# A sparse expert feed-forward: routed pairs only, with the routing of twelve batches inside the cross-attention

## The reference

```python
shared_out = _silu_and_mul(xf @ shared_w1.T) @ shared_w2.T
probs = jax.nn.softmax(xf @ gate_w.T, axis=-1)
routing_weights, selected = jax.lax.top_k(probs, 6)
combine = zeros((T, E)).at[arange(T)[:, None], selected].add(routing_weights)
gate_up = jnp.einsum('th,eoh->teo', xf, w1)
act = _silu_and_mul(gate_up)
moe_out = jnp.einsum('te,tei,ehi->th', combine, act, w2)
return moe_out + shared_out
```

## Time and profile before

| | us |
|---|---|
| median of 3 runs | 2852.18 |
| lowest and highest | 2844.84, 2854.74 |
| the profiled execution | 2846.44 |
| its span, first to last instruction | 2844.6 |

### The profile page before, as it was taken

One profiled execution on the slowest core, in us unless ns is written; L12 is line 12 of the kernel. 1 busy time (PEld: TensorE's weight loads), 2 busy tenths in 40 slices (PEclk: granted clock), 3 DMA queues, 4 the chain that ended last, 5 costly groups with the idle time before them and its releaser, 6 DMA issues. The chain is left out here.

```text
span 2844.6 us, 47270 instructions
## 1 busy us (share of the span) xinstructions
PE 2504.3 (88%) x16594; PEld 1576.6 (55%) x16594; DVE 1849.0 (65%) x3898; ACT 1520.0 (53%) x2785; POOL 442.6 (16%) x689
## 2 busy tenths in 40 slices
PE   6999999999976677778777699799989989999998
PEld 3766767676753344444444455455557655555555
DVE  5878777777747999999999322466657722223222
ACT  3666565666643699999999411466656621111110
POOL 1121212122110212222222100111113300000000
PEclk9999999999997899988999899899999989999999
DMA  5000000000000899999999600400000011111110
GB/s 192 1 1 0 0 0 0 0 0 0 0 19 27 163 187 180 184 186 176 180 184 189 121 0 1 142 1 1 1 7 14 9 45 49 38 60 37 60 41 30
DMA packets 512762, 179.54 MB, mean 63 GB/s; under 512 B 471316, under 2 KB 499216, under 8 KB 511824
## 3 DMA queue, kind: packets, MB, share of 16 engines
q1 hardware_dynamic: 512176, 177.11, 31.0%
q10 hardware_dynamic: 416, 0.16, 0.0%
HBM read 57.54 MB, written 2.23 MB: 21 GB/s over the span
## 5 line engine op out<-in xcount | busy, mean ns | idle before, releaser
L1651 DVE TENSOR_SCALAR_CACHE_REDUCE x_row<-x_p_s,x_nsq 128x1024 f32<-128x1024 f32 x512 | 621.5, 1273 | 24.1 <-PE x_p_s L1427 24.0
L1520 ACT ACTIVATE x_ints<-x_row,x_nb 128x2048 uint16<-128x2048 f32 x256 | 511.6, 1999 | 44.4 <-DMA x_turned<-x_ints 27.8
L1427 PE MATMUL x_p_s<-x_kT,x_qz 128*128 128x512 bf16 x1024 | 316.9, 405 | 132.0 <-DVE x_row L1651 128.5
L2598 DVE TENSOR_TENSOR f_h<-f_act_g,f_p_u 128x512 f32<-128x512 f32 (+1 forms) x132 | 90.8, 688 | 505.7 <-PE f_p_y L2500 484.8
L2543 ACT ACTIVATE f_act_g<-f_p_g 128x512 f32<-128x512 f32 (+1 forms) x132 | 78.8, 597 | 550.8 <-PE f_p_g L2488 550.8
L2488 PE MATMUL f_p_g<-f_xT,f_wg 128*128 128x512 f32 x528 | 251.8, 599 | 1.2 <-ACT f_xT L2527 1.2
L2488 PE MATMUL f_p_u<-f_xT,f_wu 128*128 128x512 f32 x528 | 249.4, 595 | 0.0
L2500 PE MATMUL f_p_y<-f_wd,f_h 128*128 128x256 f32 (+1 forms) x1056 | 249.0, 379 | 0.0
L2500 PEld LDWEIGHTS f_p_y<-f_wd,f_h 128*128 128x128 f32 (+1 forms) x1056 | 200.5, 190 | 82.3 <-issue 61.3
L1427 PEld LDWEIGHTS x_p_s<-x_kT,x_qz 128*128 128x128 bf16 x1024 | 72.5, 101 | 267.5 <-DVE x_row L1651 241.9
L363 POOL TENSOR_TENSOR a_rstd<-a_ssq,neghalf 128x16 f32<-128x16 f32 x32 | 125.9, 3934 | 523.1 <-DVE a_ssq L874 523.1
(11 more groups left out here) (338 smaller groups left out, 4629.3 us busy)
## 6 DMA issues: line engine op xcount, KB each, us to landing
f_share<-f_kept SPq DMA_DIRECT2D x32, 256.0 KB, 3.2
x_turned<-x_ints SPq DMA_TRANSPOSE x224, 4.8
f_share<-f_kept SPq DMA_DIRECT2D x16, 224.0 KB, 3.0
f_share<-f_kept SPq DMA_DIRECT2D x16, 192.0 KB, 2.7
f_wg<-in_L_ffn_w_dram SPq DMA_DIRECT2D x2, 1408.0 KB, 7.2
f_wu<-in_L_ffn_w_dram SPq DMA_DIRECT2D x2, 1408.0 KB, 8.1
f_wd<-in_L_ffn_w_dram SPq DMA_DIRECT2D x1, 2816.0 KB, 11.6
f_share<-f_kept SPq DMA_DIRECT2D x16, 160.0 KB, 2.5
```

Of the source, the lines that this page charges most:

```text
L1427: mm = pe.matmul(p_s[n % SLOTS][:, c * BANK:(c + 1) * BANK], qz[b % 2][:, par, a, :], kT[:, a, at:at + BANK], start=True, stop=True)
L1520: act.activation(ints[k][:, :], rows[k][:, :, :].rearrange("p s n -> p (s n)"), ACT.Exp, bias=nb[:, k:k + 1], scale=-1.0, accum_out=esum[: ...
L1651: dve.tensor_scalar(rows[k][:, half, :], p_s[n % SLOTS][:, :], nsq[:, b % 2, h:h + 1], HIGHEST, ALU.mult, ALU.min, accum_out=(low if half ...
```

## The change

**The expert part of the feed-forward is made by pair.** Each chosen pair of token and expert becomes a row in a table in DRAM, `spread`: the token's 256 numbers, its number, and its 16 weights (273 numbers, `WIDE`). An expert owns 2176 consecutive rows (`CAP`); a token's row goes to the expert's next free one. POOL writes with an indirect transfer, whose 128 target rows are read from a column of `slots`: for each batch of 128 tokens there are 6, one for each choice. Then 111 tiles (`TILES`) of 128 rows are worked, each of one expert: (12288 + 16 x 127) / 128, the most that 16 experts can need. All 111 are worked whatever the counts. Sixteen further indirect writes put rows of zeros with dump numbers behind each expert's last row.

The class `Router` holds the choice as before (`shifted`, `exponentials`, `choose`), and new steps: `positions` (a running count over the experts), `rank` (two products on PE that count earlier tokens), `take` and `number` (the slots), some 15 small DVE instructions.

**Twelve batches are routed inside the cross-attention.** `EarlyRouting` adds pieces to `CROSS_ORDERS`, for the three groups of batches 0 to 11: turns and logits on PE (`r_turn`, `r_logits`), copies on ACT, the choice on DVE once in 4 batches, `r_stage` on ACT (one staged row for each token of a batch, in one of six places in the idle self-attention's `s_kz`), and `scatter0` to `scatter5` on POOL.

**The feed-forward**, now `routed_feed_forward`, starts with the shared part alone, 3 column tiles in 4 groups, in the order 3, 0, 1, 2 of the groups, and routes and scatters group 3 beside it: 24 indirect writes, then the 16 of zeros. DVE makes tables of the tiles (row and expert of each), which PE turns. Group sums with x are stored to one of two accumulators in DRAM. Behind it the 111 tiles run in rounds, with lags 0 to 3.

```diff
 CROSS_ORDERS = {
...
-    "pool": [("spread1", 1), ("residual", 0), ("root_qk", 0), ("spread0", 0), ("norm_root", 3)],
+    "pool": [("spread1", 1), ("scatter3", 9), ("residual", 0), ("root_qk", 0), ("scatter4", 9), ("spread0", 0), ("scatter5", 9),
+            ("norm_root", 3), ("scatter0", 8), ("scatter1", 8), ("scatter2", 8)],
...
+                    pool.indirect_dma_start(s.weights.spread, bass.IndirectOffsetOnAxis(ap=s.weights.slots[:, b, k:k + 1], axis=0),
+                                            s.staged[b % n], None).then_inc(s.spread_in[b % n], 16)
...
+            sp.wait_ge(ahead.loaded, ahead.all_in)
+            early.all_in(sp)
...
+            for i in range(TILES):
+                after(sp, act_up, i - XR + 1)
+                at = sp.value_load(row_of[0:1, i:i + 1], min_val=0, max_val=SLOTS - P)
+                sp.dma_start(rows[i % XR][:, :], spread[bass.ds(at, P), :]).then_inc(rows_in[i % XR], 16)
...
+            pool.wait_ge(acc_in, 16 * (2 * groups + 2))
+            for i in range(TILES):
+                pool.wait_ge(yt_up, i + 1)
+                pool.wait_ge(ids_up, i + 1)
+                if i >= 2:
+                    pool.wait_ge(*done_of(i - 2))
+                pool.indirect_dma_start(acc[i % 2], bass.IndirectOffsetOnAxis(ap=ids[i % YR][:, :], axis=0),
+                                        yt[i % YR][:, :], None, compute_op=ALU.add).then_inc(acc_done[i % 2], 16)
...
+            def hidden(i):
+                pe.wait_ge(rowsT_up, i + 1)
+                after(pe, act_up, i - 1)
+                e = held[i]
+                for t in range(KT):
+                    mm = pe.matmul(p_g[i % 2][:, 0:2 * EI], rowsT[i % 2][:, t * P:(t + 1) * P],
+                                   weights.w1[:, t, bass.ds(e * (2 * EI), 2 * EI)], start=(t == 0), stop=(t == KT - 1))
+                mm.then_inc(gu_made, 1)
+                number_of(i + 1)
...
+            rounds([("turn_rows", 0), ("hidden", 1), ("turn_act", 2), ("result", 3)],
+                   {"turn_act": turn_act, "turn_rows": turn_rows, "hidden": hidden, "result": result}, TILES)
...
+            rounds([("rows", 0), ("silu", 1), ("result", 3)], {"rows": rows_up, "silu": silu, "result": result_up}, TILES)
...
+            rounds([("back", 2), ("weigh", 1), ("owners", 1), ("combined", 1)],
+                   {"back": act_back, "weigh": weigh, "owners": owners, "combined": combined}, TILES)
```

More of the change, by code:

```diff
@@ L2237, in small_attentions @@
         other = SmallAttention(core, ctx, "c1", cross_weights, banks, CROSS_VALUES_LAST, ahead_of_it=own)
+        early = EarlyRouting(core, ctx, own, own_weights, other, ahead)
         block = ctx.enter_context(nc.Block())
@@ L2681, in loads @@
-        yield (wd[:, wide // P:wide // P + whole, :],
-               A["L1_ffn_shared_w2"][0:whole * P, :].rearrange("(k p) h -> p k h", p=P))
-        yield wd[0:SI - whole * P, wide // P + whole, :], A["L1_ffn_shared_w2"][whole * P:, :]
-    return Weights(core, ctx, "f1", wide + SI, loads, experts=True)
+            for j, dst in enumerate((self.sg, self.su)):
+                self.loads.append((dst[:, t, :], A["L1_ffn_shared_w1"][rows, j * SI:(j + 1) * SI]))
+            self.loads.append((self.w1[:, t, :].rearrange("p (e i) -> p e i", e=EXPERTS), A["L1_ffn_w1"][rows, :, :]))
@@ new lines, in __init__, with load @@
+        self.loads += [(dst[:, :], A[name]) for dst, name in ((self.earlier, "c_earlier"), (self.first_slot, "c_first_slot"),
+                                                              (self.token, "c_token"), (self.place, "c_place"))]
+        sem = semaphores(nc, ctx)
+        self.loaded, self.ones_up = sem("f1_weights_in"), sem("f1_ones_up")
+        self.all_in = 16 * len(self.loads)
+    def load(self, eng):
+        for dst, src in self.loads:
+            eng.dma_start(dst, src).then_inc(self.loaded, 16)
```

647 lines of the change are left out of this document (620 added, 27 removed), and 1 row of the table CROSS_ORDERS.

## The result

| | us | runs | ratio to before, 95% interval |
|---|---|---|---|
| before | 2849.68 | 6 | |
| after | 2860.87 | 6 | 1.0041 [1.0027, 1.0054] |
| after, profiled: its span | 2858.4 | | before: 2844.6 |

The account below looks back on a forecast made before the run. PE was taken to bound the feed-forward (busy 527.6 of 527.7 us). Cross-attention +48 and feed-forward -94 gave -46: 2846.44 to 2800, with 5.7 for the runs' median 2806 us; range 2728 to 2905.

Parts of the forecast that it names:

- D = 1.3: Time in us for which one indirect write holds POOL, put together as 0.55 + 0.78.
- Routing alone: Cross-attention, before the first scatter: 3 us of PE over five batches and 3 of DVE's choice, 6 us more.
- Seven batches with scatters: Cross-attention: writes make root_qk late and each batch 3.2 us longer, 22 us, and 3 for later choices.
- The end: Cross-attention: twelve writes behind the last norm, 12 x 1.3, and 2.1 for landing, less 0.9: 17 us.
- The shared part: Feed-forward's start: PE through after 73.4 us, first rows loaded at 77.9 us.
- up to D = 1.36 PE ends later: Feed-forward: POOL's 40 writes are complete before PE needs the first rows if each holds POOL at most 1.36 us.
- T = 3.0: Feed-forward: time in us of each of 111 row tiles, 2.64 for PE's work and a third of the register load.
- The load's third: Row tiles: the expert number's register load on PE costs a third of 1.05 us per tile.
- Scatter-adds cost nothing, and the last 38 us: Feed-forward: scatter-adds free except the last, 4.9 us; then 23 for reading back, 5.9 last group, 4.4 store.
- POOL is the bound: Slower rival, chance 0.16: a write holds POOL 2.4 us, cross-attention +100, spread complete 42 us late, 2900 us.
- POOL is held by DVE: Slower rival, chance 0.05: writes meeting DVE's SBUF instructions lose 1.8 us each, 85 us in the cross-attention, 2891 us.
- the tile's round is long: Slower rival, chance 0.10: register load drains PE's queue in full, a row tile takes 3.7 us, +78, 2884 us.

Follow-up runs that it names:

- e3: Changed kernel with the cross-attention's 72 indirect writes issued in the feed-forward instead and scatter-adds without the add; cross-attention 38.8 us longer than before the change.
- e6: e4 with two routing pieces moved on ACT, exponentials behind turn_out and staging behind the logits' copy; 2845.90 us, ratio 0.9996.
- e1: Changed kernel, but POOL waits after every third of the feed-forward's 40 indirect writes for one more column tile; 2828.74 us, ratio 0.9944.
- e4: Changed kernel with the cross-attention's six writes placed three in each of POOL's two gaps; 2805.95 us, in later sets 2847.96 and 2845.17.
- e12: e10 without register loads on PE, expert i modulo 16 as a constant (output not the reference's); 2801.99 us against 2801.31.
- set 2: Second group of kernels measured together on one chip, with late signals: changed kernel 2858.22 us, e4 2847.96, e5 2824.68, e6 2845.90.
- e9: e6 with the 16 empty writes held until the shared part's last product is done; 2839.54 us, ratio 0.997.
- e5: e4 with a pause after every fourth of the 40 feed-forward writes until one more column tile is done; 2824.68 us, ratio 0.9926.
- e7: e6 with a pause after every third of the 40 feed-forward writes, as in e1; 2819.82 us, ratio 0.9895.
- e10: e6 with the first 12 of the 40 feed-forward writes in a row, then fours for each column tile; 2809.64 us, ratio 0.9873, again 2801.31.
- sets 1 and 5: The first and last of five groups of kernels measured together on one chip; e4 took 2805.95 us in the first, e10 2801.31 in the last.

## Why the prediction failed, step by step

- **D = 1.3** for a write: right, 1.27. But no run shows that a write's cost is made of a power's fixed price and an add over 256 columns, from which it was put together; that the sum fits may be luck.
- **Routing alone, "6 us"** with 3 more for later choices: wrong, 39 measured in e3 (30 in the batches, 9 behind the last). Of the 30, 3.8 are the first batch's, from the changed merge on DVE, and 18 stand in the two batches with a choice and the two behind them. The sum counted DVE's surplus work over its idle time. "ACT gets 1.2 us a batch beside 35% of idle time: nothing" is the sentence that failed: `r_exp` waits 2.84 us for DVE, PE waits 2.89 us behind it, and its next projection takes 1.8 us more. An in-order queue passes on a wait whatever its idle share. How the rest of the 18 divides between DVE and ACT's queue was not shown (e6). "PE 0.68 a batch" was near (0.85).
- **Seven batches with scatters, "22 us"**: 13 (e1 against e3, both without late signals) and 5 more with them. A circle was rightly expected, but at the wrong place: `root_qk` still waited 1.34 us for ACT, and `spread1` was late.
- **The end, "17 us"**: 25 (e4 against e3). The twelve writes came as forecast, 2358.84 to 2373.95; then POOL stood 8.63 us, not 2.1, until the barrier opened. No run shows what those 8.63 us are made of.
- **The shared part, "73.4 us" and 77.9 to the first rows**: this is the step that turned the sign. Without late signals it takes 84.6 (e4_order, 2367.01 to 2451.61). Of the 6.7 too many, 0.9 are in the wait for rows (5.41, with 4.5 forecast), and 3.5 are the waits of 1.16 us at the three later group turns, for which the sum had no term. With late signals PE's 36.8 us of standing still come on top. The cover, "up to D = 1.36 PE ends later" (by the sum's own terms 1.31 to 1.35), asked only whether POOL is through in time, not what its burst does to PE's signals meanwhile: those signals had no term at all.
- **T = 3.0**: 2.83. The load's third, 0.35, is nothing (e12). The rest was 0.2 too small: the four records of the result take 1.15 us, not 0.86: 0.53 for the two with 128 rows of contraction and 0.62 for the two with 48, to the start of the next piece. In the kernel after:

```profile
2602.24 1.35 PE L3217 MATMUL f_p_g<-f_w,f_rowsT 128*128 x4
...
2603.64 0.60 PE L3232 MATMUL f_p_y<-f_w,f_actT 128*128 x2
2604.17 0.70 PE L3233 MATMUL f_p_y<-f_w_low,f_actT_low 48*128 x2
2604.79 0.44 PE L3203 MATMUL f_p_x<-ident,f_rows 128*128 128x128 f32 x2
```

- **Scatter-adds cost nothing, and the last 38 us**: right; in the tiles POOL waits for ACT, not for landings, and the end took 5 us less.

The terms come to this: 82 - 48 = 34 us more in the cross-attention. In the feed-forward 45 more to the first rows, 16 less in the tiles, 5 less at the end: 24. Together 58, and with the 1.9 us of later start the 60 by which the span misses its forecast. 37 of them are the hole, about 5 late signals in the cross-attention. Without late signals the changed kernel would start its feed-forward at 2376 us (e1) and then need 84.6 + 353: about 2814 us of span, 31 less than before. So the hole alone turned a gain, a third below the forecast one, into a loss. This is an estimate from e1, e4 and the changed kernel's rest; no set showed it.

**The rivals.** "POOL is the bound", "POOL is held by DVE" and "the tile's round is long" all fell: D was 1.27 and T 2.83. The slower side came about by a mechanism that none of them named. Of the second, a trace shows a little. A write right behind another instruction of POOL took 1.01 to 1.06 us instead of 0.96 when no DVE operation that reads and writes SBUF ran beside it, and mostly 1.16 to 1.27 when one did (1.17 and 1.23 at 2247.52 and 2242.00 above): 0.1 to 0.2 us. That DVE is the reason is not shown: e3's first write in the feed-forward took 1.26 us with none beside it. The Trainium skill (SBUF — State Buffer, "SBUF: two separate sides") tells of a write that grew from about 620 to 3100 ns beside DVE; no write of this trace comes near that.

## What to carry to other kernels

A wait put into an in-order queue costs what stands behind it, whatever the engine's idle time; place new work in a gap whose next reader is late anyway (six writes in POOL's two gaps cost 0, with four of them in front of `spread1` they cost 2.7 us in a batch without a choice). A long run of back-to-back indirect writes by POOL beside PE work is worth breaking up by waits on that work's own progress: 12, then fours, gave 2810 us where the unbroken run gave 2845 in the same set (with e6's order on ACT besides, which made 2 us in set 2). Pieces added to one merged sequence can reorder others: look for a changed order on an engine before the first new piece. And when a file's time differs between sets of measurements while the kernel before doesn't, look at who waits for "remote" and how many records the profile has before explaining the difference by an edit.

## What the runs showed of the hardware that was not expected

- While POOL issues indirect writes back to back, PE's semaphore increments can reach their waiters 1 to 36 us late; of ACT's and DVE's no recorded one was. With late signals it began 13 to 16 us after the burst's first write, grew, and ended 5 to 7 us after the start of its last (4.8 in e9, 6.8 in the changed kernel). The changed kernel had it in all four of its measurements. That the burst is needed is shown by e5, e7 and e10, in which pauses alone shorten the hole of 37 us to 12.6, 2.2 and 2.2. It is not sufficient: sets 1 and 5 had none, even beside 112 writes in a row. What differs between the sets, and what holds the increments, stays open; whether POOL's issuing or the traffic of its writes does it was not tried. The one thing seen to differ is what the profile records (146 products of PE, 50501 against 50647 instructions). Every execution on record was itself recorded, with a span and a granted clock, so that the recording has a part in the lateness is an untested rival.
- Behind the last indirect write of the cross-attention the barrier opened 8.63 us later, in every run that has writes there; in e3, which has none, it opened 2.61 us after POOL's last instruction.
- A pause of PE of 2.89 us was followed by matmuls at a granted clock of 0.50 for some 4 us: 3.78 instead of 1.99 us for the same projection (e3). The stall cost 1.8 us more than its length.
